# Block products for half of product one of two row tiles, and shorter sums ahead of the ones products

## The reference, cut to what matters

```python
def fake_quant(x, scale, zp):
    q = clip(round(x / scale + zp), 0, 255)
    return (q - zp) * scale
x = x + tanh(g_xattn) * (fake_quant(layernorm(x)) @ fake_quant(ctx))
weight = U * S[None, :] @ V.T          # U, V: 2048 x 512
x = x + tanh(g_ffn) * (layernorm(x) @ weight.T)
```

## Time and profile before

| | |
|---|---|
| median of 3 runs | 584.3 us (584.17 to 584.48) |
| profiled execution, its own time | 585.77 us |
| its span, first to last instruction | 584.0 us |
| PE busy | 566.4 us (97%) |
| DVE busy | 450.7 us (77%) |
| ACT busy | 251.9 us (43%) |
| POOL busy | 197.0 us (34%) |

### The profile page before, as it was taken

One profiled execution on the slowest core, in us unless ns is written; L12 is line 12 of the kernel. 1 busy time (PEld: TensorE's weight loads), 2 busy tenths in 40 slices (PEclk: granted clock), 3 DMA queues, 4 the chain that ended last, 5 costly groups with the idle time before them and its releaser, 6 DMA issues.

```text
span 584.0 us, 7494 instructions
## 1 busy us (share of the span) xinstructions
PE 566.4 (97%) x2672; PEld 258.7 (44%) x2672; DVE 450.7 (77%) x795; ACT 251.9 (43%) x282; POOL 197.0 (34%) x146
## 2 busy tenths in 40 slices
PE   1999999999999999999999999999999999999997
PEld 0444444444444444444444444444444444444444
DVE  6878889998978851777879799789598986889222
ACT  4899978823214534537883612103530135003200
POOL 2999750000650038836643720210044005310000
PEclk9999999999999999999999999999999999999999
DMA  8999995638458997899986262423854087403712
GB/s 276 387 387 386 344 265 135 127 108 216 109 160 166 257 175 209 263 196 378 269 207 172 62 137 56 121 78 75 217 106 143 2 183 160 126 1 73 162 55 108
DMA packets 146997, 103.00 MB, mean 176 GB/s; under 512 B 109840, under 2 KB 110096, under 8 KB 146960
## 3 DMA queue, kind: packets, MB, share of 16 engines
q1 hardware_dynamic: 137968, 85.22, 56.0%
q10 hardware_dynamic: 8992, 17.30, 9.8%
HBM read 58.99 MB, written 16.78 MB: 130 GB/s over the span
## 4 chain that ended last, share of the span: by engine, by line
PE 78%; DMA 7%; DVE 6%; ACT 4%; issue 2%; ACTq 1%; POOL 1%; SPq 1%; DVEq 0%
PE bank L761 15%; PE bank L653 14%; PE bank L698 12%; PE bank L811 8%; PE bank L812 8%; PE bank L816 8%; PE bank L766 8%; DMA stage<-in_ctx_dram 3%; ACT u8r L925 2%; DMA xT<-xs 2%; PE bank L612 2%; PE bank L728 2%; DMA ring<-in_x_dram 2%; ACTq L932 1%; DVE xn L1543 1%
## 5 line engine op out<-in xcount | busy, mean ns | idle before, releaser
L299 POOL TENSOR_SCALAR ring<-ring,bvec 128x2048 f32<-128x2048 f32 x16 | 34.5, 2156 | 254.9 <-DVE bvec L1326 254.9
L653 PE MATMUL bank<-q,qT 128*128 128x512 f16 x448 | 104.2, 382 | 0.0
L761 PE MATMUL bank<-v_hl,xT 128*128 128x512 f16 x448 | 101.3, 379 | 0.0
L304 POOL TENSOR_TENSOR ring<-ring,corr 128x512 f32<-128x512 f32 x64 | 87.6, 1398 | 19.2 <-ACT corr L1040 18.2
L293 POOL TENSOR_SCALAR q<-u8r,const 128x1024 f16<-128x1024 uint8 x52 | 68.2, 1321 | 37.7 <-ACT u8r L925 33.5
L811 PE MATMUL bank<-u_hl,hbuf 128*128 128x512 f16 x208 | 78.9, 379 | 0.0
L812 PE MATMUL bank<-u_hl,hbuf 128*128 128x512 f16 x208 | 78.8, 379 | 0.0
L996 ACT ACTIVATE ln<-ln,const 128x1 f32<-128x1 f32 x16 | 4.7, 294 | 152.0 <-DVE ln L1485 151.6
L653 PEld LDWEIGHTS bank<-q,qT 128*128 128x128 f16 x448 | 44.2, 99 | 53.8 <-issue 1.4
L761 PEld LDWEIGHTS bank<-v_hl,xT 128*128 128x128 f16 x448 | 43.8, 98 | 52.4
L1559 DVE SCALAR_TENSOR_TENSOR ring<-bank,cy,ring 128x512 f32<-128x512 f32 x63 | 46.0, 744 | 14.1 <-PE bank L816 14.1
(11 more groups left out here) (200 smaller groups left out, 833.8 us busy)
## 6 DMA issues: line engine op xcount, KB each, us to landing
out_dram<-ring SPq DMA_DIRECT2D x63, 256.0 KB, 3.5
ring<-in_x_dram SPq DMA_DIRECT2D x62, 256.0 KB, 4.4
v_hl<-in_ctx_dram SPq DMA_DIRECT2D x26, 512.0 KB, 11.5
stage<-in_ctx_dram ACTq DMA_DIRECT2D x17, 512.0 KB, 5.9
u_hl<-in_L_ffn_V_dram SPq DMA_DIRECT2D x8, 512.0 KB, 11.5
corr<-in_ctx_dram ACTq DMA_DIRECT2D x8, 512.0 KB, 7.1
stage<-in_ctx_dram SPq DMA_DIRECT2D x6, 512.0 KB, 11.4
q<-in_ctx_dram ACTq DMA_DIRECT2D x4, 512.0 KB, 11.6
```

Of the source, the lines that this page charges most:

```text
L304: nc.gpsimd.tensor_tensor(xq(t, n), xq(t, n), corr[:, n * W:(n + 1) * W], ALU.add).then_inc(x1_pre, 1)
L653: mm = nc.tensor.matmul(unit_bank(t, n)[:, :], qT_of(t)[:, k, :], q2[:, n, k, :], start=(k == 0), stop=(k == KT - 1))
L761: nc.tensor.matmul(h_bank(u)[:, :], x_home(u, g)[:, half, k % 8, :], v_hl[:, k, 0, :], start=(g == 0 and a == 0 and half == 0), stop=False)
```

## The change

- **Tiles 6 and 7, columns 2 and 3** are made by seven block products (`late_product`), columns 0 and 1 as before. Three T sums are written over the context blocks they come from, the fourth (`l_t1`) into `xT`, the S sums into `xs`. PE's new order is (6, 0), (6, 1), P1, P2, `mm3(5)`, (7, 0), P5, P6, P3, P7, (7, 1), P4. Seven adds (`late_add`) replace four evictions. The products use banks 5 to 7, which `mm4(4)` waits for.
- **Column sums**: an eighth step (`k_fold`) adds the two halves and a constant `C_MID` to centre the result; PE multiplies once per block; the correction uses the bias `C_AFS` for it.
- **ACT's order**: `op1` of chunks 12 to 15 with their refills (17 to 20) later; chunk 16 ahead of `x_hi_half(7, 0)`; `x_hi_half(7, 1)` ahead of the refills of the rooms and of chunk 17; chunks 26 and 27 ahead of `sums1(8)`; `hid_hi(7)` between `quantise(8)` and `op2(8)`.
- **Waits**: GpSimd's chunks of columns 2 and 3 and the refills of the rooms wait for all seven products.

```diff
-    KS = CQ - 1
+    KS = CQ
-        MIXED = [(6, 0), (6, 1), (7, 0), (6, 2), (6, 3), (7, 1), (7, 2), (7, 3)]
+        MIXED = [(6, 0), (6, 1), (6, 2), (6, 3), (7, 0), (7, 1), (7, 2), (7, 3)]
...
+        l_seq = {k: i + 1 for i, k in enumerate((P1, P2, P5, P6, P3, P7, P4))}
+        l_bank = lambda k: bank[{P2: 7, P5: 6, P3: 6}.get(k, 5)]
+        l_t1 = t1_room
+        l_s = [xs[:, 0, 0, :], xs[:, 0, 1, :], xs[:, 1, 1, :], xs[:, 1, 0, :]]
...
@@ GpSimd, op2 @@
-                if b > 0:
-                    pool.wait_ge(s1_done, s_unit(TB * b - 1, n) + 1)
+                if b > 0 and n < 2:
+                    pool.wait_ge(s1_done, s_unit(TB - 1, n) + 1)
+                elif b > 0:
+                    pool.wait_ge(l_done, NP)
@@ SP, h_transpose @@
                 elif u == 5:
-                    sp.wait_ge(s1_done, S1_END(6))
+                    sp.wait_ge(l_done, NP)
@@ PE @@
-                for a in range(CK):
-                    mm = nc.tensor.matmul(colsum_bank(1, n)[:, :], ones_h[:, :], k_sums(n)[:, a * W:(a + 1) * W],
-                                          start=(a == 0), stop=(a == CK - 1))
-                mm.then_inc(colsum_done, 1)
+                nc.tensor.matmul(colsum_bank(1, n)[:, :], ones_h[:, :], k_sums(n)[:, 0:W], start=True, stop=True)\
+                    .then_inc(colsum_done, 1)
...
+            def late_product(k):
+                a, b = LATE
+                left, right = {P1: (a_part(a, 0), b_part(2, 0)), P2: (a_part(a, 1), b_part(2, 1)),
+                               P5: (l_s_part(0), t_part(l_t1)), P6: (l_s_part(1), b_part(2, 0)),
+                               P3: (l_s_part(2), b_part(3, 1)), P7: (l_s_part(3), b_part(3, 0)),
+                               P4: (a_part(b, 1), b_part(2, 1))}[k]
+                if k == P1:
+                    pe.wait_ge(y_ready, NQ * EARLY[0])
+                elif k == P5:
+                    pe.wait_ge(l_s_made, 1)
+                    pe.wait_ge(l_t1_made, 2)
+                elif k == P6:
+                    pe.wait_ge(l_s_made, 2)
+                    pe.wait_ge(l_read, l_seq[P1])
+                elif k == P3:
+                    pe.wait_ge(l_s_made, 3)
+                    pe.wait_ge(l_read, l_seq[P5])
+                elif k == P7:
+                    pe.wait_ge(l_s_made, 4)
+                    pe.wait_ge(l_read, l_seq[P6])
+                elif k == P4:
+                    pe.wait_ge(l_t4_made, 2)
+                    pe.wait_ge(l_read, l_seq[P7])
+                for i in range(KH):
+                    mm = nc.tensor.matmul(l_bank(k)[:, :], left[:, i, :], right[:, i, :],
+                                          start=(i == 0 and k in (P1, P2, P5)), stop=(i == KH - 1),
+                                          skip_group_check=k in (P6, P7, P4, P3))
+                mm.then_inc(l_done, 1)
...
+                    if u == EARLY[0] and n < 3:
+                        pe.wait_ge(l_read, l_seq[(P3, P2, P4)[n]])
...
@@ ACT's list @@
-            stream(12, 14)
+            for i in range(12, 16):
+                op1(CB + i)
             root2(7)
+            op1(CB + 16)
             x_hi_half(7, 0)
-            stream(14, 17)
-            act.wait_ge(s1_done, S1_END(TB - 1))
+            for i in range(12, 16):
+                refill(NEXT[CB + i])
+            x_hi_half(7, 1)
+            act.wait_ge(l_done, NP)
             for i in range(4):
                 refill(CB + ORDER.index(f"room{i}"))
-            x_hi_half(7, 1)
             stream(17, 22)
             hid_hi(6)
-            stream(22, 26)
+            stream(22, 28)
             sums1(8)
-            stream(26, 30)
+            stream(28, 30)
             quantise(8)
+            hid_hi(7)
             op2(8)
             stream(30, 32)
-            hid_hi(7)
@@ DVE @@
+            def late_t3():
+                dve.wait_ge(e_done, NP)
+                for c in range(2):
+                    b12, b22 = [k_piece(flat2(b_part(3, h)), c, 2 * HW) for h in range(2)]
+                    tt(b12, b22, b12, ALU.subtract).then_inc(l_t3_made, 1)
...
+            def late_t1():
+                dve.wait_ge(mm3_half, 2 * EARLY[1] + 2)
+                for c in range(2):
+                    dve.wait_ge(l_t2_made, c + 1)
+                    tt(k_piece(l_t1, c, 2 * HW), k_piece(flat2(b_part(3, 1)), c, 2 * HW),
+                       k_piece(flat2(b_part(2, 0)), c, 2 * HW), ALU.subtract).then_inc(l_t1_made, 1)
...
+            def k_fold(n):
+                dve.wait_ge(k_summed, KS * n + CQ - 1)
+                left, right = k_sums(n)[:, 0:W], k_sums(n)[:, W:2 * W]
+                stt(left, left, C_MID, right, ALU.add, ALU.add).then_inc(k_summed, 1)
@@ DVE's list @@
             x1_units(6, (0, 1))
+            late_t3()
             row_correction(7)
+            middle()
+            late_add(P1)
+            late_t2()
+            late_add(P2)
+            late_s_sums()
             hid_lo(5)
-            x1_unit(7, 0)
-            x1_units(6, (2, 3))
-            stats2(6)
+            late_t1()
+            late_t4(0, 1)
+            late_add(P5)
+            late_t4(1, 2)
+            late_add(P6)
+            x1_evict(7, 0)
+            late_add(P3)
+            x1_stats(7, 0)
+            variance2(6)
+            late_add(P7)
+            scale2(6)
             x_lo_half(6, 0)
-            x1_unit(7, 1)
+            x1_evict(7, 1)
+            late_add(P4)
             x_lo_half(6, 1)
-            x1_units(7, (2, 3))
-            stats2(7)
+            x1_stats(7, 1)
+            late_stats(7, 2, P4)
+            variance2(7)
             y_unit(4, 0)
+            scale2(7)
             x_lo_half(7, 0)
...
-            k_sum_part(0, 6)
+            k_sum_part(0, 6, 7)
             y_unit(5, 0)
+            k_sum_part(0, 7)
+            k_fold(0)
...
             quantise(8)
             k_sum_part(1, 3)
-            k_sum_part(2, 1, 6)
+            k_fold(1)
+            k_sum_part(2, 1, 4)
             hid_lo(7)
             row_correction(8)
             y_unit(6, 0)
+            k_sum_part(2, 4, 6)
             y_unit(6, 1)
             k_sum_part(2, 6)
+            k_fold(2)
```

More of the change, by code:

```diff
@@ L881, in _ @@
             mm3(4)
-            for i, (t, n) in enumerate(MIXED):
-                if i == 2:
-                    mm3(5)
-                s1_part(t, n)
+            s1_part(6, 0)
+            s1_part(6, 1)
+            late_product(P1)
+            late_product(P2)
+            mm3(5)
+            s1_part(7, 0)
+            late_product(P5)
+            late_product(P6)
+            late_product(P3)
+            late_product(P7)
+            s1_part(7, 1)
+            late_product(P4)
             mm4(4)
@@ L1271, in constants, with middle @@
                 dve.wait_ge(const_ready, 1)
+            def middle():
+                step(ts(C_MID, C_NC2, -float(KT), -255.0 * KT / 2, ALU.mult, ALU.add))
+                step(ts(C_MIDP, C_MID, -float(P), None, ALU.mult))
+                stt(C_AFS, C_MIDP, C_AF1, C_AFF, ALU.mult, ALU.add).then_inc(mid_ready, 1)
             def largest_s():
@@ L1777, in _ @@
             k_sum_part(3, 6)
+            k_fold(3)
             y_unit(7, 2)
```

66 lines of the change are left out of this document (60 added, 6 removed).

## The result

The changed kernel took 589.1 us (median of 5, 588.51 to 589.83) against 584.2 for the kernel before in the same runs: a ratio of 1.0083 (95% interval 1.0073 to 1.0094), 0.8% slower. The prediction of 585.0 was 4.1 us too low, and its upper end of 588.0 did not hold the time. The profiled execution took 589.83 at a span of 588.0, 4.0 more than the span of before.

A forecast was written before the change was run, and what follows sets the result against it. TensorE's matmuls plus waits were taken as the bound. Fewer products, the old wait gone and new waits summed to +0.7 us, taking the profiled execution from 585.77 to 586.5; the median, 1.47 lower, was forecast at 585.0, range 581.3 to 588.0.

The forecast's parts named there:

- The old wait: TensorE's one wait after the start, for VectorE's `y_unit(5, 0)`, was to go: -1.41 us.
- The products: TensorE: eight fewer products in tiles 6 and 7, -1.73 us; four fewer ones products, -0.65 and later -0.2.
- The first wait: TensorE before P5 waits for VectorE's `late_t1`, done at 234.9 against 233.3: 1.7 us.
- The second wait: TensorE before the fourth unit of `mm4(4)` waits for `y_unit(4, 0)`, which starts at 255.5: 1.35 us.
- P7's 0.1: TensorE, ready for P7 at about 240.1, waits 0.1 us for VectorE's add of P6.
- The third wait: TensorE at the third ones product (302.7) waits for VectorE's `k_fold(2)`, done at 304.2: 1.6 us.
- With 0.5 idle gone and 0.5 for the later data: ScalarE up to `sums1(8)`: two extra chunks at 1.75 each, these two 0.5 us corrections, start at 283.1 for 279.71.
- Full granted clock in every slice: Opening reading of the profile page: TensorE busy 97% of the span, at 2.4 GHz in every slice.
- GpSimd out of the way: Rival, 0.28: `late_t2` and `late_t4` pieces at 1.13, 582.8 us; sign: `y_unit(4, 0)` ends by 255.
- No third wait: Rival, 0.10: `sums1(8)` ready 1.6 us sooner, no wait at the third ones product, 583.4 us.
- Late refills: Rival, 0.25: refills in saturated DMA delay `sums1(8)`, 587.2 us, or 588.2 with dearest pieces; sign: room 3 lands after 278.
- signs of being wrong: `late_t1` ends before 233.3, `y_unit(4, 0)` before 255, `quantise(8)` not waiting for ScalarE, or rooms operations waiting for data.

The follow-up runs named there:

- the ones edit alone: The kernel before with only one operand at the ones (`k_fold`, `middle`, one product per block), no block products and ScalarE's order as before: 583.48 us, ratio 0.9987.

## Why the prediction was wrong

**The old wait (-1.41), and the median.** It went, but it had never been in most executions. The prediction took the wait off and then took 1.47 off again to come to the median, although that 1.47 was the same hole. On its own terms the forecast should have been 0.7 + 1.4 above the median, 586.4. This is 1.4 of the miss of 4.1. The rest, below, is against the profiled execution (586.5 predicted, 589.83 measured, itself 0.7 above its median).

**The products (-1.73, -0.65, -0.2).** Right.

**The first wait (1.7).** Right: 1.64. That is luck in part: `middle` cost 2.15 for 0.75, `late_t2` 4.05 for 5.13 and `late_t1` 2.35 for 2.8, and these errors nearly cancel. They are not independent: with `middle` moved away, `late_t2` took 4.85. The Trainium skill (SBUF — State Buffer, Who interferes with whom) says that a VectorE instruction with two SBUF inputs and a GpSimd instruction that reads SBUF shut each other out for a whole instruction. The last step of `middle`, one column with two inputs, agrees: it began 0.12 behind GpSimd's row instruction and ended with it, at 221.99.

```profile
220.00 1.97 POOL L315 TENSOR_SCALAR ring<-ring,bvec 128x2048 f32<-128x2048 f32 x1 [8.20 <-DVE bvec L1392]
```

Its two single-input steps took 0.14 and 0.15, and in the kernel with `middle` later the last one, at 270.06, took 0.22. For `late_t4` the same rule gave 2.3 a piece and the prediction 1.9; the rows show 1.22 and 1.40 here, and 1.22 to 2.06 over the kernels of this study. The rule's bound held; where between two chunks a piece falls may decide its cost below that, but no run tests it.

**The second wait (1.35).** In place, at half its size (0.69): `y_unit(4, 0)` started at 254.34 for 255.5. The cheaper `late_t4` put P6's add 0.9 ahead of the forecast, but of that only 0.4 was left at `x_lo_half(6, 0)` (245.22 for 245.6); the other 0.8 is this half itself, 2.7 for 3.5. P7's 0.1 did not occur.

**The third wait (1.6): this is the step that failed, together with the clock behind it.** The third ones product starts when VectorE has done `k_fold(2)`: at 304.2 by the prediction, at 305.8 in the trace. These 1.6 us have two sources of like size.

- `quantise(8)` came at 288.67 for 287.8. The two chunks ahead of it were counted rightly, as the run with them alone shows. "With 0.5 idle gone and 0.5 for the later data", nothing net, was not: ScalarE lost 3.0 us between chunk 17 and `sums1(8)` to its own DMA issues (0.92 and 0.62 for 0.37 before) and to late data (the rooms landed a median of 13.6 us after issue for 11.6). With the refills at their old place this stretch took 18.2 for 21.05. Most of it stayed hidden, since ScalarE reached chunk 17 at 262.89 for the 265.1 of the prediction: two errors of 3.0 and -2.2, of which 0.8 is left at `sums1(8)` (283.94 for 283.1).
- From there to the end of `k_fold(2)` VectorE took 17.1 us for 16.3.

The prediction also named one place where TensorE waits, and there are two: `y_unit(6, 0)` stands behind `hid_lo(7)` in that chain and was done at 300.1, so the fourth unit of `mm4(6)` waited 1.81 ahead of the 2.71. This hole adds nothing of its own. VectorE's chain never waits for TensorE there, so without it TensorE would have come to the third ones product 1.81 sooner and waited 4.5 in one piece. The two holes are 4.5 in sum for 1.6 since VectorE was 1.6 later and TensorE 1.3 earlier than predicted: without the first hole it would have arrived at 301.4, for 302.7, mostly because its waits before were 0.8 shorter.

**The clock: missing from the prediction.** "Full granted clock in every slice" was read as a property of the kernel. It was one of a TensorE that hardly paused. A wait was priced at its length alone, and behind this one the clock cost 1.7 more. In the profiled execution the late fold and the clock are the whole miss: 586.5 + 1.6 + 1.7 = 589.8.

**The rivals.** GpSimd out of the way was half right on the pieces, and by its own sign it stood on the line: `y_unit(4, 0)` ended at 255.0. No third wait: wrong. Late refills named the side that came, and its mechanism is there, 3.0 us on ScalarE; behind the earlier start only 0.8 of it reached `sums1(8)`. Its sign, room 3 landing after 278, did not come (ScalarE read that room at 277.19, having waited 0.88 for it), but one of the prediction's signs of being wrong did: operations on rooms waited for their data.

**What stays open.** Why the late end costs 3.8 with the block products and 2.6 without: VectorE's extra work and ScalarE's refills were not told apart. Also what, beside a pause, makes the clock fall. Removing the wait before P5 did not gain (586.14 for 585.27); that VectorE's and ScalarE's chain takes it back is read from one profile of each. The best version seen is the ones edit alone, 583.48.

## What to carry to other kernels

When a helper engine's work moves later, follow its whole list and ask of every item who waits for it, not only of the last. One delay can open several holes; if the helper's chain never waits in turn, their sum is how late its last item is, and taking one hole away moves its length to the next. Look for the clock behind each hole, in windows of 2 us: where it fell, it cost 1.3 to 1.7 us on top. Treat that as a risk and not as a price, since it came behind 1.99 us and stayed away behind 3.12. An edit that moves VectorE's work beside another of GpSimd's instructions changes the cost of the rest: `middle` freed 2 us, and 1.75 of them were paid again. Before you take credit for a wait that goes, check that the profiled execution's own time is near the median; if it lies above by about that wait, the wait is likely that execution's alone.
